# Feed-forward pieces in another order on VectorE, ScalarE and GpSimd, in a gated cross-attention block

## What is computed

```
x = x + tanh(g_xattn) * xattn(layernorm(x), ctx, itok)
x = x + tanh(g_ffn)   * ffn(layernorm(x))
```

```
h = silu(bitlinear(x, w1, b1))     # 256 -> 1024
h = gelu(h)
h = layer_norm(h, ln_g, ln_b)
y = bitlinear(h, w2, b2)           # 1024 -> 256
```

## Time and profile before

| what | value |
|---|---|
| median of 3 runs | 251.32 us (251.13 to 251.66) |
| the profiled execution's own time | 251.6 us |
| its span, first to last instruction | 249.8 us |
| around the span | 1.8 us |
| busy: TensorE, VectorE, ScalarE, GpSimd | 210.2, 187.7, 155.6, 149.7 us |
| mean granted TensorE clock | 0.937 |

### The profile page before, as it was taken

How to read it: one execution, slowest core, us unless ns; L and a number is a source line. 1 busy time by engine, 2 the same in 40 slices (tenths; PEclk the granted TensorE clock), 3 DMA queues, 4 the chain that set the end, 5 groups by cost and what they waited for, 6 DMA issues and landing times.

```text
span 249.8 us, 4518 instructions
## 1 busy us (share of the span) xinstructions
PE 210.2 (84%) x1452; PEld 167.5 (67%) x1452; DVE 187.7 (75%) x430; ACT 155.6 (62%) x455; POOL 149.7 (60%) x222
## 2 busy tenths in 40 slices
PE   1799899999999999998998999899899746834453
PEld 1677788688978877886786888678678632513231
DVE  2587556689786679988988998898899842779761
ACT  2256627737557597759559875965887593849021
POOL 0415726639776469788787878778787832062630
PEclk9999999999999999999999999999999996775557
DMA  6999994000000000000000000000000000000001
GB/s 194 286 213 184 318 385 189 0 0 3 1 3 0 3 3 0 3 0 0 24 1 0 25 0 0 4 21 0 4 22 0 3 0 21 0 0 0 24 22 31
DMA packets 11357, 12.40 MB, mean 50 GB/s; under 512 B 3936, under 2 KB 10336, under 8 KB 11104
## 3 DMA queue, kind: packets, MB, share of 16 engines
q1 hardware_dynamic: 10432, 11.44, 16.6%
q10 hardware_dynamic: 896, 0.61, 0.8%
HBM read 11.00 MB, written 1.05 MB: 48 GB/s over the span
## 4 chain that ended last, share of the span: by engine, by line
PE 45%; DVE 19%; POOL 12%; issue 11%; ACT 9%; DMA 1%; DVEq 0%; SPq 0%; POOLq 0%
PE bank_pair L805 7%; PE bank_score L883 5%; PE bank_ff L920 4%; POOL h_small L430 4%; PE bank_lat L907 4%; PE bank_swap L808 3%; DVE z L1206 3%; PE bank_prob L895 3%; DVE h L1230 3%; POOL prob_room L485 3%; DVE neg_max L1289 3%; ACT prob_room L654 3%; PE bank_ff L959 3%; PE bank_ff L939 2%; POOL qcat L408 2%
## 5 line engine op out<-in xcount | busy, mean ns | idle before, releaser
L654 ACT ACTIVATE prob_room<-bank_score,neg_max 128x128 f32<-128x128 f32 x128 | 45.3, 369 | 23.5 <-DVE neg_max L1289 23.5
L485 POOL TENSOR_TENSOR prob_room<-prob_room,rsum 128x512 f32<-128x512 f32 x32 | 33.3, 1041 | 26.0 <-DVE rsum L1297 25.8
L406 POOL TENSOR_TENSOR qcat<-qcat,turned 64x256 f32<-64x256 f32 x32 | 30.8, 963 | 11.9 <-DVE turned L1141 11.8
L883 PEld LDWEIGHTS bank_score<-kcat,qcat 128*128 128x128 f32 x256 | 33.7, 192 | 2.3
L805 PE MATMUL bank_pair<-qcT,wcat 96*128 96x128 f32 x256 | 34.0, 276 | 0.0
L883 PE MATMUL bank_score<-kcat,qcat 128*128 128x128 f32 x256 | 33.7, 275 | 0.0
L642 ACT COPY probT_room<-bank_prob 128x512 f32<-128x512 f32 x32 | 19.0, 594 | 22.4 <-PE bank_prob L895 22.4
L920 PE MATMUL bank_ff<-m_sb,latT 128*128 128x256 f32 x128 | 31.9, 395 | 0.0
L805 PEld LDWEIGHTS bank_pair<-qcT,wcat 96*128 96x128 f32 x256 | 31.1, 192 | 0.4 <-DVE wcat L1126 0.2
L408 POOL TENSOR_TENSOR qcat<-qcat,turned 64x256 f32<-64x256 f32 x32 | 29.6, 924 | 2.5
L1137 DVE TENSOR_TENSOR qcat<-bank_pair,cst 128x512 f32<-128x512 f32 x32 | 21.6, 674 | 10.5 <-PE bank_swap L808 10.5
(11 more groups left out here) (163 smaller groups left out, 436.6 us busy)
## 6 DMA issues: line engine op xcount, KB each, us to landing
wo<-in_L_xattn_W_o SPq DMA_DIRECT2D x1, 2048.0 KB, 19.5
w_sb<-in_L_ffn_w SPq DMA_DIRECT2D x2, 1024.0 KB, 9.9
out_x<-y SPq DMA_DIRECT2D x8, 128.0 KB, 1.7
wuq<-in_L_xattn_W_uq SPq DMA_DIRECT2D x1, 768.0 KB, 11.5
ctx_all<-in_ctx ACTq DMA_DIRECT2D x2, 256.0 KB, 5.0
x_all<-in_x SPq DMA_DIRECT2D x2, 256.0 KB, 4.7
cst<-in_consts SPq DMA_DIRECT2D x1, 512.0 KB, 7.0
x_all<-in_x SPq DMA_DIRECT2D x1, 512.0 KB, 8.2
```

The source lines that it names most:

```text
L406: nc.gpsimd.tensor_tensor(odd, odd, add_odd, ALU.add).then_inc(pair_half, 1)
L485: nc.gpsimd.tensor_tensor(p, p, rsum[:, k % 2, :].unsqueeze(2).broadcast_to([P, GROUP, kts * P]), ALU.mult).then_inc(prob_scaled, 1)
L654: last = nc.scalar.activation(prob_of(n, kts)[:, j, :], src[:, j, :], ACT.Exp, bias=neg_max[:, k % 2, j:j + 1], accum_out=esum[:, k % 2, j ...
L883: last = nc.tensor.matmul(bank[:, j * kts * P:(j + 1) * kts * P], qcat[:, k, hh // 2, hh % 2, :], kcat[:, b, hh % 2, 0:kts * P], start=Fal ...
```

## The change

The queries are rotated in place as before. No instruction of the computation is added or taken away; pieces change their place in the programs of three engines.

- VectorE: `residual_and_quantise(f-1)` in step 2 is cut in two: `residual` stays in step 2, `quantise_x` goes to step 3. `moments_h(f-2)` follows it there. `output` goes from the end of step 3 (tile f-3) to step 0 of the next tile, behind `turn_step` and ahead of `layer_norm_h`.
- ScalarE: `sum_squares(f-3)` in step 1 goes ahead of `copy_probT`; `tanh(f-2)` in step 1 goes ahead of the exponentials; `gelu(f-2)` goes from the end of step 2 to step 3, between `copy_probT` and `copy_h(f-3, 1)`.
- GpSimd: `root_hq(f-3)` goes from the end of step 1 to its start, ahead of `normalise`; `dequantise_x(f-1)` goes from step 2 to step 3.

```diff
@@ GpSimd
             def feed_forward(f, k):
                 if k == 1 and there(f, 3):
-                    root_hq(f - 3)
                     dequantise_h(f - 3)
                 if k == 2 and there(f, 1):
                     root_x(f - 1)
+                if k == 3 and there(f, 1):
                     dequantise_x(f - 1)
...
                 for k in range(STEPS):
+                    if k == 1 and there(f, 3):
+                        root_hq(f - 3)
                     if step_no(f, k) >= 1:
                         normalise(*behind(f, k, 1), kts)
@@ ScalarE
                             copy_latT(*behind(f, k, lag + 1))
+                        if k == 1 and there(f, 3):
+                            sum_squares(f - 3)
                         if step_no(f, k) >= lag:
                             copy_probT(*behind(f, k, lag), kts)
                         if k == 0 and there(f, 2):
                             copy_x1(f - 2)
+                        if k == 1 and there(f, 2):
+                            tanh(f - 2)
+                        if k == 3 and there(f, 2):
+                            gelu(f - 2)
                         if k == 3 and there(f, 3):
                             copy_h(f - 3, 1)
-                        if k == 1 and there(f, 3):
-                            sum_squares(f - 3)
                         if f < F:
                             exponentials(f, k, kts)
                         prepare(f, k)
-                        if k == 1 and there(f, 2):
-                            tanh(f - 2)
                         if k == 2 and there(f, 3):
                             copy_h(f - 3, 0)
-                        if k == 2 and there(f, 2):
-                            gelu(f - 2)
@@ VectorE
+            x_amax = {}
+
+            def quantise_x(c):
+                quantise(xl[:, :], xs, x_amax[c], x_floor, x_scale, c + 1, xq_ready)
+
-            def residual_and_quantise(c):
+            def residual(c):
...
-                quantise(xl[:, :], xs, absmax(xl[:, :], xs), x_floor, x_scale, c + 1, xq_ready)
+                x_amax[c] = absmax(xl[:, :], xs)
...
             def feed_forward(f, k):
+                if k == 0 and there(f, 4):
+                    output(f - 4)
                 if k == 0 and there(f, 3):
                     layer_norm_h(f - 3)
...
                 if k == 2 and there(f, 1):
-                    residual_and_quantise(f - 1)
-                if k == 3:
-                    stages = [(moments_h, 2), (output, 3)]
-                    if f == F - 1:
-                        stages.reverse()
-                    for stage, lag in stages:
-                        if there(f, lag):
-                            stage(f - lag)
+                    residual(f - 1)
+                if k == 3 and there(f, 1):
+                    quantise_x(f - 1)
+                if k == 3 and there(f, 2):
+                    moments_h(f - 2)
...
                 def after():
                     invert_sums(F - 1, STEPS - 1)
+                    output(F - 4)
                     first_product(F - 2)
                     layer_norm_h(F - 3)
-                    residual_and_quantise(F - 1)
+                    residual(F - 1)
+                    quantise_x(F - 1)
                     moments_h(F - 2)
```

## The result

The changed kernel takes 258.89 us (median of 4 runs, 258.42 to 260.7) beside 251.49 us of the kernel before on the same chip: a ratio of 1.0288 with a 95% interval of 1.021 to 1.0366. It is 7.4 us slower. 257.3 was forecast against a median of 251.32, with a range of 254.3 to 260.0.

A forecast was written before the change was run, and what follows sets the result against it. TensorE, the busiest engine, was taken as the late one. Span 249.8, plus 7.4 for the tiles and loop end, less 1.4 for the clock, plus 1.8 around it gave 257.6; the median 0.28 lower: 257.3 us, range 254.3 to 260.0.

The forecast's parts named there:

- `output` behind `turn_step`: Step 0, tiles 4 to 7: `up` on TensorE waits for `y_done` at T+5.00, a new wait of 1.26 us.
- The rope add beside it: GpSimd's L406 beside L1264 of `output` in step 0: costs VectorE 0.20 us, with 0 and 0.40 as bounds.
- `sum_squares` ahead of `copy_probT`: Step 1: the copy now waits for `h_ready`, and `values` behind it, a new wait of 0.80 us.
- gelu ahead of `copy_h`: Step 3: `down` waits 1.30 us in place of the 1.17 before `values`; the step is 0.13 longer.
- `root_hq` first: GpSimd, step 1: the floor is there at T+11.1, so `quantise_h` waits no more, 0.72 us saved on VectorE; step 2 -0.07.
- `normalise` has slack: GpSimd: behind the roots `normalise` is done by T+13; its reader L895 comes at T+14.2.
- A table switch: Rival, ScalarE: 1.4 us of emptying beside the load makes `down` later in tiles 3 to 7: +7, 264 us; chance 0.02.
- The rival of the clock inside the loop: TensorE's idle pieces bring 1.2 GHz to a stretch of each of tiles 4 to 7, 2.8 us each: 268 us; chance 0.04.
- behind the loop L895 can follow L907 at once: -1.26: Behind the loop: the 1.19 us wait of L895 for `normalise` goes, as `output` is behind it now: -1.26 us.
- The term for the clock behind it: Behind the loop, up to the last `attn_out`: no gain or -2.8 us from TensorE's clock, taken as -1.4.
- The faster rival: VectorE's floor waits (0.72, 0.89 us) set TensorE's pace, the three new waits do not bind: some -8, 243 us; chance 0.03.

The follow-up runs named there:

- e1: The changed kernel with `output` alone put back to the end of step 3: 254.64 us.
- e5: The changed kernel with `output` still in step 0, but ahead of `turn_step` instead of behind it: 254.45 us.
- e9: The changed kernel with `sum_squares` directly behind `copy_probT`, still ahead of `tanh`: 256.16 us.
- e10: The changed kernel with `output` back at the end of step 3 and `sum_squares` between `copy_probT` and `tanh`: 251.55 us, ratio 1.0009 to the kernel before.
- e12: The kernel before with `root_hq` alone moved to the head of GpSimd's step 1: 247.60 us.
- e2: The changed kernel with `sum_squares` alone put back behind `copy_h(f - 3, 1)`, and so behind `tanh`: 270.99 us.
- e4: The changed kernel with `output` back at the end of step 3 and `sum_squares` behind `tanh`: 262.98 us.
- e6: The kernel before with only `root_hq` first on GpSimd and `quantise_x`, `dequantise_x` in step 3: 247.45 us.
- e3: The changed kernel with `gelu` alone put back to the end of step 2: 253.32 us.
- e11: Kernel before with `root_hq` first, `quantise_x`, `dequantise_x` in step 3, and step 2's maxima ahead of `quantise_h`'s last three pieces: 242.45 us.

## Why the prediction was right

The forecast's mechanism held in each step of the middle tiles, and only in part behind the loop. In profiled spans, 7.2 us were lost where 6.0 were summed (7.4 without the clock, less 1.4):

| part | forecast | measured |
|---|---|---|
| before tile 2 | 0 | -0.47 |
| tile 3 | +1.1 | +1.27 |
| tile 4 | +2.23 | +2.52 |
| tile 5 | +2.23 | +2.23 |
| tile 6 | +2.23 | +2.25 |
| tile 7 | +0.89 | +0.89 |
| end of loop to L897 | -1.26 | -0.71 |
| from there to the last `attn_out`: the clock | -1.4 | -1.05 |
| behind it | 0 | +0.27 |

- **`output` behind `turn_step`.** Step 0 was to be 1.46 longer and is 1.55 longer. e1 and e5 show that it is this wait, and e5 that the wait of `up` hangs on the place behind `turn_step` and not on the step.
- **The rope add beside it.** 0.20 was taken between 0 and 0.40: L1271 took 0.17 more. The Trainium skill's rule that the loser of the shared port pair fully blocks ("SBUF — State Buffer", glossary) would hold L1271 until L406 ends at 170.67 and let it end near 171.15; it ended at 170.96. It is the same 0.66 in tiles 4 to 7. The measurement lies between no block and that rule, and decides.
- **`sum_squares` ahead of `copy_probT`.** `values` was to start at T+9.80 and did at T+9.89. Its wait is 0.65 and not 0.80, since TensorE came later. e9 shows the cause.
- **gelu ahead of `copy_h`.** `down` at step start +5.38, measured 189.19 - 183.80 = 5.39. The wait of 1.17 was replaced by one of 1.32. e10 shows it with the other two new waits gone. As a price of the move, though, the 0.13 of the sum is too small: with `root_hq` first, gelu in its old place and no other new wait, step 3 takes 5.54 (e12), 0.74 less than it does here. The sum came out because it set both moves together against the kernel before.
- **`root_hq` first.** `quantise_h` was to reach its wait at T+13.9 and find the floor there; L1192 starts at T+13.96 without a wait. The statement that `normalise` has slack held here (it ends at T+12.35, its reader comes at T+14.27), but not with `sum_squares` behind `tanh` (e2). Step 2 was to be 0.07 shorter and is 0.16 shorter; with step 0 0.09 too long the two misses cancel, and a tile's 2.25 for 2.23 is in part luck.
- **A table switch** took its load and nothing more: L644 ends at 186.20, the load starts at 186.21. The drain that the Trainium skill counts beside it ("ScalarE: Activation LUTs", "What ACT_TABLE_LOAD costs") shows in none of these rows, and the rival built on it is out.
- **The rival of the clock inside the loop** did not come about in the changed kernel (clock 1.00 from tile 2 to the end of tile 7), but in e1, e2 and e4 the clock did fall in some tiles.

The size was a little low, by 1.2 in spans. Tile 4 has a delay of 0.28 that its neighbours do not have: L644 started 0.37 after L897's end there instead of 0.09. It is no accident of that execution: step 3 of tile 4 takes 6.55 or 6.56 for 6.28 in all seven kernels that have gelu ahead of `copy_h` in step 3 (the changed one, e1, e2, e4, e5, e9, e10), and in none of the others. What causes it stays open.

The term "behind the loop L895 can follow L907 at once: -1.26" was mis-sized: it does follow at once, but L907 itself (now L909) already ran at 1.2 GHz and took 1.05 instead of 0.58 to the next. The clock fell before the gap ahead of it, behind the wait of 2.29 of the last `down`. In the kernel before it was still up at 207.23, though `values` of the last tile had waited 2.51. This took 0.5 of the 1.26. The term for the clock behind it, -1.4, was the middle between two ends, and the measured -1.05 is no clock that stayed up: it was down for L909 and L897 and came back earlier, so that the 16 L922 took 3.69 us at 1.00, where in the kernel before they took 4.74 at 0.78. That the two are close is luck. In the last stretch the granted clock was 0.54 for 0.62, which stands beside the +0.27. The -0.47 before tile 2 is no part of the change: tile 2 begins between 73.14 and 74.34 in the profiled executions of all 14 kernels.

The faster rival is refuted as put, and yet part of its observation was sound: VectorE's wait for the floor of `quantise_h` did set TensorE's pace. Without it, and without the new waits, the change would have been 4.2 us faster than the kernel before (e6), about half of the 8 that the rival summed: the wait before `values` fell from 1.17 to 0.57 and no further. The point where it was to decide, `y_done` before T+3.78 and `h_ready` before T+7, does not decide it alone. e10 has both (T+1.3 and T+6.97) and is 4.1 us above e6: `down` waits 1.32 in each middle tile there, behind gelu. No run moves `tanh` alone; but e3 keeps it ahead of the exponentials, and its steps 2 and 3 (4.86 and 5.07) are as short as those of e11, so it costs nothing there.

## What to carry to other kernels

Of a piece moved in an in-order queue, ask first what wait stands just ahead of it in its new place, and which other engine waits for the piece: both costs here (`output` behind the wait for the same step's projection, the copy behind `sum_squares`) can be read from the rows of before, to a tenth of a microsecond. Split a change of order into its moves and time each: here one move gained 3.7 us (e12) and lay hidden under the others, of `output`, `sum_squares`, gelu and `tanh`, that together cost 11 (the changed kernel against e6). When a wait is gone, look for what gates the start of that chain (here the maxima behind `quantise_h`), since pulling the gate forward paid where moving the chain's own pieces did not.

## What the runs showed of the hardware that was not expected

The granted clock of TensorE may fall behind a single short gap inside a busy loop, and may not. In e1, in tile 3, `values` waited 1.63 us, and after it part of the work ran at 1.2 GHz. The rows are TensorE's, then the stretch behind them with the columns of the earlier trace rows:

```profile
98.07 0.65 PE L909 MATMUL bank_lat<-probT_room,kvc 128*64 128x256 f32 x4 [1.63 <-ACT probT_room L644]
...
100.62 1.83 PE L885 MATMUL bank_score<-kcat,qcat 128*128 128x128 f32 x8
```

```profile
98.00:102.30 4.30, 4.23 (x18) 2.78 (x19) 4.26 (x6) 2.89 (x12) 3.85 (x3) 0.60 0.00 0
```

In the changed kernel the same wait of 1.63 stands at the same place, L885 behind it takes 1.05 us as ever, and the clock stays at 1.00:

```profile
97.48 0.65 PE L909 MATMUL bank_lat<-probT_room,kvc 128*64 128x256 f32 x4 [1.63 <-ACT probT_room L644]
...
99.15 1.05 PE L885 MATMUL bank_score<-kcat,qcat 128*128 128x128 f32 x8
```

```profile
98.00:102.30 4.30, 3.82 (x30) 3.23 (x29) 4.26 (x5) 2.88 (x11) 3.46 (x4) 1.00 0.00 0
```

In e2 the same wait before `transpose_probs` stands in tiles 4, 5 and 6 (1.93, 1.93 and 1.94 us): the clock fell behind the first and the third and stayed at 1.00 behind the second. In e4 it fell behind 1.63 in tile 3 and 2.09 in tile 4. A fall cost 1.6 us in e2 (tile 6 with it 27.36 us, tile 5 without it 25.74), and so makes a tile's length scatter where its order of work does not. In the changed kernel, in e3 and in e5 to e12 the granted clock is 1.00 over the whole stretch from 73 to 195 us. What decides between a fall and none these runs do not show.
